# Causal stage of a two-layer attention/FFN kernel: another order of the same work on VectorE, TensorE, ScalarE and GpSimd

## The reference, cut to what matters

```python
x = x + _L0_xattn_ref(_layernorm(x), ctx, ctx, mask)              # 16 sequences of 128 tokens, width 256
x = x + _L0_ffn_ref(_layernorm(x), ...)                           # 2 of 4 encoder layers per sequence: 32 "units"
x = x + _L1_xattn_ref(_layernorm(x), ctx, ctx, Wq, bq, ..., Wo, bo)   # 16 heads, causal softmax
x = x + _L1_ffn_ref(_layernorm(x), ...):
    x1 = einsum('btd,hd->bth', x, sw1) + sb1;  x2 = einsum('btd,hd->bth', x, sw2) + sb2
    sh = _ln(silu(x1) * x2, s_ln_g, s_ln_b)
    shared_out = einsum('bth,dh->btd', sh, sw3) + sb3
    # and for 512 listed tokens: one of 8 experts, mixed with shared_out, written over it
```

## Time and profile before

| | us |
|---|---|
| three timed runs | 845.12, 848.23, 848.43 (median 848.23) |
| the profiled execution's own time | 846.53 |
| span of its trace | 844.7 |
| mean granted TensorE clock | 0.931 of full |
| busy share: PE, DVE, ACT, POOL | 86%, 74%, 40%, 45% |

### The profile page before, as it was taken

How to read it: one execution, slowest core, us unless ns; L and a number is a source line. 1 busy time by engine, 2 the same in 40 slices (tenths; PEclk the granted TensorE clock), 3 DMA queues, 4 the chain that set the end, 5 groups by cost and what they waited for, 6 DMA issues and landing times.

```text
span 844.7 us, 29095 instructions
## 1 busy us (share of the span) xinstructions
PE 724.6 (86%) x10986; PEld 576.8 (68%) x10986; DVE 627.9 (74%) x1799; ACT 337.9 (40%) x710; POOL 376.9 (45%) x647
## 2 busy tenths in 40 slices
PE   5679469999999999999999999997878787764497
PEld 4567457888888878888888888774545555543286
DVE  4686556787887888887887878778678787865645
ACT  4656224434344443434444344443434344441210
POOL 2788722435444353534535354533243433335043
PEclk9876589999999999999999999999889999995599
DMA  7677300000000000000000000002121212113010
GB/s 268 226 243 230 138 2 2 3 3 3 2 4 2 3 3 3 3 3 2 3 3 3 3 2 10 9 28 83 32 71 51 83 48 86 45 64 100 13 38 7
DMA packets 24367, 40.72 MB, mean 48 GB/s; under 512 B 3695, under 2 KB 16633, under 8 KB 23979
## 3 DMA queue, kind: packets, MB, share of 16 engines
q1 hardware_dynamic: 22808, 36.86, 13.2%
q0 software_dynamic: 704, 1.71, 0.7%
q10 hardware_dynamic: 726, 0.30, 0.2%
HBM read 30.34 MB, written 8.91 MB: 46 GB/s over the span
## 4 chain that ended last, share of the span: by engine, by line
PE 63%; DVE 18%; POOL 8%; issue 7%; ACT 3%; DMA 0%; POOLq 0%; DVEq 0%; ACTq 0%
PE ps L480 7%; PE ps L474 6%; PE ps L482 6%; PE ps L481 6%; PE ps L669 5%; DVE mx L1427 4%; PE ps L725 3%; PE ps L687 3%; PE ps L727 3%; PE ps L726 3%; PE ps L616 3%; POOL rs L1828 2%; POOL w_lo L1853 2%; PE ps L618 2%; PE ps L723 2%
## 5 line engine op out<-in xcount | busy, mean ns | idle before, releaser
L1060 ACT ACTIVATE pT<-ps 128x1024 f32<-128x1024 f32 x96 | 93.1, 1021 | 135.7 <-PE ps L669 135.7
L1427 DVE TENSOR_REDUCE mx<-ps 128x16 f32<-128x2048 f32 x48 | 109.4, 2280 | 2.9 <-PE ps L639 2.9
L725 PE MATMUL ps<-xh,w_hi 128*128 128x128 bf16 x512 | 99.4, 219 | 0.0
L726 PE MATMUL ps<-xl,w_hi 128*128 128x128 bf16 x512 | 99.3, 219 | 0.0
L727 PE MATMUL ps<-xh,w_lo 128*128 128x128 bf16 x512 | 99.2, 219 | 0.0
L1914 POOL TENSOR_TENSOR y<-y,vec 128x256 f32<-128x256 f32 x32 | 23.2, 726 | 170.0 <-DVE y L1201 170.0
L1826 POOL TENSOR_TENSOR rs<-mv,cst 128x1 f32<-128x1 f32 x132 | 27.8, 210 | 122.8 <-DVE mv L1198 117.6
L1828 POOL TENSOR_TENSOR rs<-rs,cst 128x1 f32<-128x1 f32 x132 | 73.8, 559 | 10.3
L480 PE MATMUL ps<-w_hi,hh 128*128 x256 | 69.8, 273 | 0.0
L482 PE MATMUL ps<-w_lo,hh 128*128 x256 | 69.8, 273 | 0.0
L481 PE MATMUL ps<-w_hi,hl 128*128 x256 | 69.8, 273 | 0.0
(11 more groups left out here) (350 smaller groups left out, 2470.8 us busy)
## 6 DMA issues: line engine op xcount, KB each, us to landing
stage<-in_w SPq DMA_DIRECT2D x32, 384.0 KB, 3.7
vec<-in_vec SPq DMA_DIRECT2D x4, 896.0 KB, 5.6
vec<-in_tw SPq DMA_DIRECT2D x12, 256.0 KB, 3.1
ctxc<-in_ctx SPq DMA_DIRECT2D x19, 128.0 KB, 2.6
comb<-x SPq DMA_DIRECT2D x16, 128.0 KB, 1.7
comb<-t SPq DMA_DIRECT2D x16, 128.0 KB, 1.8
shared<-x1b SPq DMA_DIRECT2D x16, 128.0 KB, 1.7
out<-x SPq DMA_DIRECT2D x16, 128.0 KB, 1.8
```

What stands on the lines that cost most here:

```text
L725: mm(dst, w(w_hi, c, j), xh[:, c, :], start=False, stop=False)
L726: mm(dst, w(w_hi, c, j), xl[:, c, :], start=False, stop=False)
L1060: A(pT[:, 8 * a:8 * a + 8, :].rearrange("p h q -> p (h q)"), ps[:, 2 * a:2 * a + 2, :].rearrange("p g k -> p (g k)"), ACT.Exp, scale=SCALE ...
L1427: nc.vector.tensor_reduce(mx[:, :], att.rearrange("p g s k -> p (g s) k"), AX.X, ALU.max, negate=True).then_inc(m_max, 1)
```

## The change

No instruction is added or removed. On VectorE `block_c` has a new order: the expert sum and `sh_zlow` first, then `qk_low`, the normalizations, `bias_v`, the maxima; `y_stats_of` goes from the block's start to its middle, and `stats_c` from the next block's start to right behind `x3`. On TensorE the masks leave `scores` and `scores_T`: `mask_rows` (four matmuls) stands ahead of `projection_v`, and three of the four `mask_columns` ahead of `shift_transpose`, with a wait for the maxima of their own. On GpSimd `x_bias` stands behind the first `rstd`, `tw` behind `sh_affine`, `y_root` last. On ScalarE `tw` stands ahead of `o_evict`.

```diff
             def scores(u, causal):
                 pe.wait_ge(qkT_hi, u + 1)
-                if causal:
-                    for g in range(4):
-                        mm(ps[:, g, :], identb[:, :], causb[:, 0:1, :].broadcast_to([128, 4, 128]), ...)
...
+            def mask_rows(u):
+                pe.wait_ge(pT_b, u)
+                for g in range(4):
+                    mm(ps[:, g, :], identb[:, :], causb[:, 0:1, :].broadcast_to([128, 4, 128]), ...)
+            def mask_columns(u, banks):
+                pe.wait_ge(m_max, u + 1)
+                for g in banks:
+                    mm(ps[:, g, :], identb[:, :], causb[:, 1:2, :].broadcast_to([128, 4, 128]), ...)
...
             def scores_T(u, causal):
+                pe.wait_ge(mT_sb, u + 1)
                 if causal:
-                    for g in (1, 2, 3, 0):
-                        if g == 0:
-                            pe.wait_ge(mT_sb, u + 1)
-                        mm(ps[:, g, :], identb[:, :], causb[:, 1:2, :].broadcast_to([128, 4, 128]), ...)
-                else:
-                    pe.wait_ge(mT_sb, u + 1)
+                    mask_columns(u, (0,))
...
             def block_c(b, slot, ex=None):          # TensorE
                     values(n, slot, 0)
                 if more:
+                    mask_rows(m)
                     if b >= 4:
                         pe.wait_ge(s_zsplit, b + (A1 - 4))
...
                     projection_v(None)
-                    pe.wait_ge(pT_b, n + 1)
                     scores(m, True)
...
                 if more:
+                    mask_columns(m, (1, 2, 3))
                     shift_transpose(m)
...
             def block_c(b, weights=None):           # ScalarE
                     sh_e(b - 2)
+                if weights is not None:
+                    tw(*weights)
                 if served(b):
                     o_evict(n)
                 if served(b - 1):
                     sh_y(b - 1)
-                if weights is not None:
-                    tw(*weights)
...
             def block_c(b, slot, ex=None, weights=None, between=None):   # GpSimd, behind rstd(1)
+                if served(b + 1):
+                    x_bias(b + 1, 1 - slot)
...
                     sh_affine(b - 3)
+                if weights is not None:
+                    tw(*weights)
+                if served(b - 4):
+                    sh_sum(b - 4)
                 if served(b + 3):
                     y_root(b + (B + 3))
-                if served(b + 1):
-                    x_bias(b + 1, 1 - slot)
-                if served(b - 4):
-                    sh_sum(b - 4)
-                if weights is not None:
-                    tw(*weights)
```

More of the change, by code:

```diff
@@ L631, in scores @@
                 pe.wait_ge(qkT_hi, u + 1)
-                if causal:
-                    for g in range(4):
-                        mm(ps[:, g, :], identb[:, :], causb[:, 0:1, :].broadcast_to([128, 4, 128]),
-                           start=True, stop=False)
                 for c in range(KC):
@@ L641, in scores @@
                 last.then_inc(s_psum, 1)
+            def mask_rows(u):
+                pe.wait_ge(pT_b, u)
+                for g in range(4):
+                    mm(ps[:, g, :], identb[:, :], causb[:, 0:1, :].broadcast_to([128, 4, 128]),
+                       start=True, stop=False)
+            def mask_columns(u, banks):
+                pe.wait_ge(m_max, u + 1)
+                for g in banks:
+                    mm(ps[:, g, :], identb[:, :], causb[:, 1:2, :].broadcast_to([128, 4, 128]),
+                       start=True, stop=False)
             def shift_transpose(u):
@@ L648, in scores_T @@
             def scores_T(u, causal):
+                pe.wait_ge(mT_sb, u + 1)
                 if causal:
-                    for g in (1, 2, 3, 0):
-                        if g == 0:
-                            pe.wait_ge(mT_sb, u + 1)
-                        mm(ps[:, g, :], identb[:, :], causb[:, 1:2, :].broadcast_to([128, 4, 128]),
-                           start=True, stop=False)
-                else:
-                    pe.wait_ge(mT_sb, u + 1)
+                    mask_columns(u, (0,))
                 pe.wait_ge(qk_split, u + 1)
@@ L786, in block @@
                     o_rows(n)
+                if causal_m:
+                    mask_rows(m)
                 scores(m, causal_m)
@@ L1604, in block_c @@
                 n, m = b + UNITS, b + (UNITS + 1)
[L1605 to L1608, removed]
+                if n - 4 < UNITS:
+                    add_expert(n - 4, at((n - 4) // 2))
+                if served(b - 4):
+                    sh_zlow(b - 4)
+                if served(b + 1):
+                    qk_low(m)
                 if served(b - 1):
                     sh_y(b - 1)
-                if n - 4 < UNITS:
-                    add_expert(n - 4, at((n - 4) // 2))
                 if n - 3 < UNITS:
@@ L1616, in block_c @@
                     sh_gnorm(b - 3)
-                if served(b - 4):
-                    sh_zlow(b - 4)
                 if served(b + 1):
                     bias_v(m, 1 - slot, vc[:, VC_V:VC_V + D])
-                    qk_low(m)
                     maxima(m)
@@ L1627, in block_c @@
                     sum2(n - 2, slot)
+                if served(b - 1):
+                    sh_low(b - 1)
+                if served(b - 4):
+                    sh_sum(b - 4)
+                if served(b):
+                    o_low(n)
+                if served(b + 3):
+                    y_stats_of(at(b + 3), b + (B + 3))
                 if served(b + 2):
                     y_low(b + (B + 2), 2 * KC)
-                if served(b - 4):
-                    sh_sum(b - 4)
[L1632 to L1635, removed]
                 if served(b - 2):
@@ L1640, in block_c @@
                     x3(n, b, slot)
+                    stats_c(b)
                 if n - 2 < UNITS:
@@ L1715, in _ @@
             y_of(at(3), B + 3, UNITS)
+            stats_c(0)
             dve.wait_ge(sv_in, 32)
```

## The result

| | before | after |
|---|---|---|
| median (lowest to highest), us | 847.1 | 804.6 (802.3 to 806.0) |
| ratio, 95% interval | | 0.950 (0.948 to 0.952) |
| the profiled execution's own time, span | 846.5, 844.7 | 804.1, 802.3 |
| mean granted TensorE clock | 0.931 | 0.940 |
| busy share PE, DVE, ACT, POOL | 86, 74, 40, 45% | 89, 77, 42, 47% |

The account below looks back on a forecast made before the run. A ring of waits bounds the causal blocks, no engine being full. Gains 19.9 + 1.6 + 1.8 (X to M), 9.8 (masks), 2.0 + 1.2 (ends) make 36.3 us, from 846.5 to 810; range 801 to 822.

Parts of the forecast that it names:

- X to M: From the start of x3 (X) to the start of the maxima (M): 4.78 us in place of 6.77, 1.99 gained a block.
- M to X: From the maxima to the next x3: three of four column masks leave the path, 0.70 us gained a block, 14 blocks.
- The gate: VectorE's sh_gate: with GpSimd's weights moved under the maxima it falls from 1.13 us to 0.29, minus 0.84.
- Rival A, the port: GpSimd's x_bias starts before VectorE's y_of and holds it on the shared port; qk_low 0.4 us late, 815; chance 0.13.
- the sign that I gave (over 0.6): On VectorE, y_of lasting over 0.6 us would show the port rival.
- the stage's end and behind it: Gain of 2.0 us before sh_out at the causal stage's end, and 1.2 from the next X to GpSimd's first gather.
- blocks 1 to 3: First causal blocks, which do not wait for sh_zlow: gain taken as 0.6 us each (bounds 0 and 1.99), 1.8 together.
- 806 to 813: The time range in which the forecast holds; chance 0.52.
- 800 to 806: Time range for the case that clock spells go and blocks 1 to 3 gain in full; chance 0.10.
- The clock: In b = 3, M to X took 10.05 us, partly at 1.2 GHz; that 2.7 may go, giving 807, but was kept.
- The bounds: Limits of the gain: 16 us (half VectorE's gain, no masks, ends 3) to 42 (blocks 1 to 3 in full), plus clock.

## Why the prediction was right

- **X to M.** 4.78 foreseen, 4.75 measured, and by the list that I gave: `hl` done at 2.37 (2.41 foreseen), `ql` released by k at 2.71 (2.73 foreseen), then VectorE's own list. The run with z's low part late shows which move carries most of it (1.21 of the 2.02), and VectorE's order alone shows that no other engine's list is needed: 10 x 2.02 = 20.2 against 19.9. VectorE keeps up as counted: the gate ends 6.42 behind M (6.5 foreseen), and x3 waits 0.25.
- **M to X.** 6.62 foreseen, 6.67 measured; 0.63 a block in place of 0.70. The term is a little too large: I divided 0.96 by four masks, and the 0.96 held a change of shape that stays. Three masks take 0.66 (665.00 to 665.66), and the run with columns late gives 0.65 to 0.66. Of the two mask moves, the columns carry it all in the kernel after, the rows nothing (804.3 without their move); the rows' move by itself in before was not run.
- **The gate.** It is at 0.29, as foreseen, but not for the reason given. I wrote that the weights' move to the maxima takes 0.84 off. VectorE's order alone takes it off too, up to b = 13. The step that failed is that one: it took the weights' place beside the gate as fixed, while both lists were about to slide against each other. So GpSimd's and ScalarE's part of the change is worth nothing in its company (803.0 without it, 804.6 with it, intervals 0.946 to 0.952 and 0.948 to 0.952), and costs 2% by itself.
- **Rival A, the port.** It did not come in the middle blocks: `y_of` had begun 0.21 earlier, as the margin said. It came in b = 2, where `y_of` lasts 0.95, the sign that I gave (over 0.6), and in b = 3, in the expert sum, which I had not counted. With `x_bias` in its old place and VectorE's order alone these blocks have 4.81 and 4.75 from X to M in place of 5.27 and 4.99: 0.7 us in all. See also t at 0.62.
- **The size.** The sum was 36.3, the traces have 42.4. The order itself gave 34.9, 1.4 less than the sum (masks 1.0, the stage's end and behind it 0.5, blocks 1 to 3 0.3 less; X to M of b = 4 to 14 0.4 more). On top come 5.5 of TensorE's lower clock in before and 1.95 ahead of the stage. The order alone would have given 846.5 - 34.9 = 811.6, 1.4 from the forecast; that the time came out 5 us under it is the clock, and a start of the stage that has nothing to do with the change. The measured time lies under the 806 to 813 to which I gave 0.52, and in the 800 to 806 to which I gave 0.10. Of that case the first half happened, the clock came back; the second did not, blocks 1 to 3 gained 1.5 and not 6.0.
- **The clock.** I saw b = 3, and kept it on purpose; I did not see that four more blocks last 14.4 to 15.2 us, because I took the block time from one full-clock block and multiplied. The list of all maxima had it.
- **The bounds.** They are added up wrongly: half of VectorE's gain and 3 at the ends is 14.7, not 16, and blocks 1 to 3 in full make 40.5, not 42. A gain of 16 would be a time of 830, outside the range of 801 to 822.

## What to carry to other kernels

Where blocks form a ring of waits, look for a short instruction that another engine waits for while it stands behind long ones whose inputs come late, and list all block times, not one: those that stick out can show what else a gap costs. A move on one engine shifts every other list against it, so a collision seen before is no longer where it was; who starts first on a shared port decides who waits. And test the halves of a change alone: the one that adds nothing in company may be harmful by itself. List the blocks at the edges as well: a collision that the middle ones have lost can stand in the first and the last.

## What the runs showed of the hardware that I had not expected

- **A gap can cost more than itself, and unused work can be worth its time.** Three matmuls that nothing reads took 9 us off the time (821.6 to 812.6; 9.4 in the M to X parts of the traces): TensorE was then granted its full 2.4 GHz in all 14 of these parts, and without them five have 0.66 to 0.81. The same filler in the same place of the kernel before, where the clock is mostly lost behind another gap, gave nothing (ratio 0.996 to 1.000). The Trainium skill, "TensorE: Matmul & The Clock Gate", section "Part 1: The HAM clock gate", has the clock follow how busy TensorE has been of late; these runs agree, and add that the place of the work matters.
- **The port's order.** These are VectorE's normalizations and its elementwise steps with both inputs in SBUF, beside GpSimd's additions and subtractions of 128 or more columns. Those that really began first kept their time (gate 0.29, `y_of` 0.41), and GpSimd's 128x256 addition grew from 0.73 to between 0.78 and 0.83; those that came later ended 0.14 to 0.16 us behind GpSimd's (the expert sum of b = 3, queued behind `y_of`, 0.28). A recorded start 0.07 ahead is not enough when the instruction before is still running (`y_of` of b = 2, 0.95). VectorE's instructions that read PSUM kept theirs (maxima 2.28 beside the weights), and so did the statistics (0.29 at 649.35, begun 0.05 behind the weights). Beside the roots' 128x1 power (0.55) nothing was held: with VectorE's order alone `y_of` begins 0.05 behind it and keeps its 0.41. The Trainium skill, "SBUF — State Buffer", section "SBUF: two separate sides", tells this as an exclusive lock that the later one waits for; the rows beside wide GpSimd instructions agree, those beside the power do not show it.
